# Projections taken term by term, and half of the values formed behind attention's first units

## The chip, the cores and the metric

The kernel runs on one core of a Trainium2 chip. Its time is the device time of one execution in microseconds. The engines are PE (matrix products), DVE and ACT (elementwise work, copies, exponentials), POOL (small elementwise work, indirect transfers) and SP (issues transfers). Each works through its own queue in order and waits on semaphores that the others raise.

## The reference, cut to what matters

Per image of 16: a layer norm, a convolutional channel attention, and then on its 1024 tokens of 192 channels the block that the change touches:

```python
qkv = jnp.einsum('btc,fc->btf', x, W_qkv)          # x: normalised tokens
wei = jnp.einsum('bqhd,bkhd->bhqk', q, k) * scale   # 6 heads of 32
wei = jnp.where(causal[None, None], wei, -jnp.inf)
wei = jax.nn.softmax(wei, axis=-1)
out = jnp.einsum('bhqk,bkhd->bqhd', wei, v).reshape(Bq, Tq, H * HS)
out = jnp.einsum('btf,cf->btc', out, W_proj) + b_proj
out = jnp.einsum('btf,cf->btc', out, W_proj) + b_proj
```

After the images, a mixture of four experts (two per token) runs over all tokens in blocks of 512 rows.

## The kernel before

Image by image, PE does the convolutions as matmuls over shifted copies (`ring`), the channel mixing of token blocks 0 to 7 into PSUM banks `k % 6`, and then attention. DVE adds a bias to each mixed block (`channel_mixed`, L1045, raises `y_sb`), takes statistics, and writes the normalised tokens `xhat`, blocks 0 to 3 in `normed(i, 0)`, 4 to 7 in `normed(i, 1)` (L1021). The fixed order on DVE is: `normed(i, 0)`, blocks 5 and 6 mixed, `low_channels(i, 0)`, block 7 mixed, `low_qk(i, 0)`, `normed(i, 1)`, the next two `low_qk`, `low_channels(i, 1)`, three more `low_qk`.

Precision comes from split operands. PE transposes the tokens (L1714); ACT copies the result as high parts `T0` and `T1` (L1458, raises `T_hi`), and DVE subtracts to get `T2` and the low rows of `T1` (`low_channels`, L1029 and L1032, raises `T_lo`). Every projection is a sum of five matmuls, `qkv` in the code: two on `T0`, one on `T2`, two on `T1`. There are six groups of 128 rows of queries and keys by 512 tokens (`queries_keys`, group `n` in bank `n % 4`; 0 to 2 are the first half of the tokens). Each is copied by ACT (`QKh`, L1551, raises `qk_hi`) and subtracted by DVE (`QKl`, `low_qk`, L1038, raises `qk_lo`). Loads issued by SP (`load_keys`) and POOL (`load_queries`) stack the parts into `KS` and `QS`. Group 1 writes bank 1, which mixed block 7 used, so from group 1 on the wait is for all eight blocks in `y_sb`.

Values are eight chunks of 128 tokens, five matmuls each (L1739), copied by ACT to `v_sb` (L1462, raises `v_done`); before, chunks 2 to 7 stand between the last group and the first score, in banks 6, 7, 4, 5 by turns.

Attention is 48 units, query chunk by query chunk, six heads each. For unit `n` PE computes the scores of unit `n + 3` (or `n + 2`), and then transposes the probabilities of unit `n` (L1782) in banks 4 and 5. DVE takes a row maximum of the scores (L1051), ACT the exponential with its row sums (L1469) and a copy of the transposed block (L1483). The first score waits for the last `qk_lo`, since scores use banks 0 to 3, and for the landed loads. The output matmuls of a query chunk (L1804) use banks 6 and 7. POOL scatters the rows of the image before (`send`, L780), issues the query loads (L357), adds a bias (`output_bias`, L786) and spreads the inverse row sums (`inverse_wide`, L728).

Of the kernel before, what the change touches and what calls it, by code (L numbers as in the profile page):

```python
# [15 lines left out]
P = 128  # L16
# [3 lines left out]
def hybrid_block_kernel(nc, x, ln_g, ln_b, conv_w, conv_bias_row, conv_taps, conv_bias, alpha_rows, w_f_t, b_f,  # L20
# [50 lines left out]
    with ExitStack() as ctx:  # L71
# [387 lines left out]
        def value_bank(k):  # L459
            return (6, 7, 4, 5)[k % 4]  # L460
# [189 lines left out]
        def _(pool):  # L650
# [138 lines left out]
            for i in range(B):  # L789
# [7 lines left out]
                if i:  # L797
                    send(i - 1, 5, 6)
# [7 lines left out]
                if i:  # L806
                    send(i - 1, 6, NC)
# [615 lines left out]
        def _(act):  # L1423
# [102 lines left out]
            for i in range(B):  # L1526
# [15 lines left out]
                for n in range(NQ):  # L1542
                    if n == QK_FIRST:
                        for k in range(2):
                            values_out(i, k)
                        high_channels(i, 1)
                    f, nh = QK_ORDER[n]
# [4 lines left out]
                for k in range(2, NC):  # L1552
                    values_out(i, k)
                for n, (qc, h) in enumerate(SOFT):
                    exponentials(i, n)
                    if n:
                        blocks_out(i, n - 1)
                    if qc and h == 2:
                        norms_out(i, qc - 1)
# [49 lines left out]
        def _(pe):  # L1609
# [110 lines left out]
            def queries_keys(i, n):  # L1720
                f, nh = QK_ORDER[n]
                if n >= 4:
                    pe.wait_ge(qk_lo, NQ * i + n - 3)
                if n < 4:
                    pe.wait_ge(y_sb, NC * i + min(NC - 1 + n, NC))
                for m, (act_part, w_part) in enumerate(qkv):
                    if f == 0 and m in (0, 3):
                        pe.wait_ge(T_hi, 4 * i + 2 * nh + 1 + m // 3)
                    if f == 0 and m in (2, 3):
                        pe.wait_ge(T_lo, 4 * i + 2 * nh + m - 1)  # L1730
                    last = t.matmul(bank(n % 4), w_part[:, P * f:P * (f + 1)],
                                    act_part[:, BANK * nh:BANK * (nh + 1)], start=m == 0, stop=m == 4)
                last.then_inc(qk_ps, 1)

            def values_of_tokens(i, k):
                if k >= 4:
                    pe.wait_ge(v_done, NC * i + k - 3)
# [5 lines left out]
            def passed(i, t):  # L1743

                if t < 2:
                    pe.wait_ge(v_done, NC * (i + 1))
# [100 lines left out]
            for i in range(B):  # L1847
# [35 lines left out]
                for n in range(QK_FIRST):  # L1883
                    queries_keys(i, n)
# [3 lines left out]
                for n in range(QK_FIRST, NQ):  # L1888
                    queries_keys(i, n)
                for k in range(2, NC):  # L1890
                    values_of_tokens(i, k)
                if not i:
# [3 lines left out]
                for n, (qc, h) in enumerate(SOFT):  # L1896
                    for m in SCORED[n]:
                        query_scores(i, m)
                    if n == NU - 1 and i + 1 < B:
# [173 lines left out]
```

## Time and profile before

| | us |
|---|---|
| median of 3 runs | 3336.41 |
| lowest, highest | 3331.54, 3340.59 |
| profiled execution | 3334.18 |
| its span, first to last instruction | 3332.3 |
| PE busy in the span | 3067.4 (92%) |
| DVE busy | 2202.3 (66%) |
| ACT busy | 1871.5 (56%) |
| POOL busy | 874.5 (26%) |

The images take the first two thirds of the span, the experts the rest. The mean granted clock is 0.984. Start times below count from the start of the span. A busy span of a matmul overlaps that of the next, so the pace of PE is read from start to start.

### The profile page before, as it was taken

The numbers are of one execution on the slowest core, as the hardware profiler recorded it, in microseconds if no ns is written. First come the engines' busy times: TensorE is split into PE (matmuls) and PEld (weight loads), VectorE is DVE, ScalarE is ACT, GpSimd is POOL, SyncE is SP. The second block draws the span as 40 slices with busy tenths as digits, with TensorE's granted clock in tenths as the row PEclk, the third lists the DMA queues.
The fourth block names the chain that finished last, engine by engine and source line by source line (L and its number), as shares of the span: only waits on it lengthen the run. The fifth ranks groups of instructions, "written<-read, shape, count | busy, mean of one in ns | idle before, by whom it ended". The sixth has DMA issues, their size and how long they took to land. (4 is left out here: it accounts for less than half of the span.)

```text
span 3332.3 us, 72396 instructions
## 1 busy us (share of the span) xinstructions
PE 3067.4 (92%) x26642; PEld 2344.2 (70%) x26642; DVE 2202.3 (66%) x5619; ACT 1871.5 (56%) x3996; POOL 874.5 (26%) x1142
## 2 busy tenths in 40 slices
PE   4999999999999999999999999958999999999995
PEld 1666667666666676666766766637888888888884
DVE  3777677677776776777767767664555655655653
ACT  0647456465474664654746647535555555555553
POOL 2121313303223133132230331450223223223222
PEclk9999999999999999999999999979999999999997
DMA  7546445454364454544644546515667767667673
GB/s 177 142 114 178 115 124 148 124 150 126 113 184 116 122 149 122 153 118 120 173 125 115 148 123 154 156 47 159 195 206 213 221 208 220 210 205 228 206 212 120
DMA packets 256516, 519.82 MB, mean 156 GB/s; under 512 B 70919, under 2 KB 161991, under 8 KB 246521
## 3 DMA queue, kind: packets, MB, share of 16 engines
q1 hardware_dynamic: 222878, 453.58, 48.6%
q0 software_dynamic: 29184, 59.81, 6.0%
q8 instruction: 217, 3.56, 0.4%
q10 hardware_dynamic: 4107, 1.81, 0.3%
q14 instruction: 130, 1.06, 0.1%
HBM read 242.82 MB, written 117.71 MB: 108 GB/s over the span
## 5 line engine op out<-in xcount | busy, mean ns | idle before, releaser
L1051 DVE TENSOR_REDUCE minus_max<-ps 128x1 f32<-128x128 f32 (+7 forms) x768 | 571.6, 750 | 243.7 <-PE ps L1772 232.3
L1469 ACT ACTIVATE p_sb<-ps,minus_max 128x128 f32<-128x128 f32 (+7 forms) x768 | 569.3, 741 | 41.3 <-DVE minus_max L1051 37.8
L1782 PE MATMUL ps<-ident,p_sb 128*128 128x128 f32 x3456 | 530.6, 279 | 44.2 <-ACT p_sb L1469 18.4
L1356 DVE TENSOR_TENSOR g_lo<-g,g_hi 128x512 fp32r<-128x512 f32 x402 | 282.8, 704 | 369.3 <-ACT g_hi L1593 369.3
L1592 ACT ACTIVATE g<-ps,bcur 128x512 f32<-128x512 f32 x402 | 276.6, 688 | 429.2 <-PE ps L1967 429.2
L1483 ACT ACTIVATE PT<-ps 128x512 f32<-128x512 f32 (+3 forms) x768 | 396.7, 517 | 132.7 <-PE ps L1782 123.5
L1782 PEld LDWEIGHTS ps<-ident,p_sb 128*128 128x128 f32 x3456 | 370.0, 141 | 99.4 <-ACT p_sb L1469 37.5
L1983 PE MATMUL ps<-w_all,g_hi 128*128 x1608 | 434.6, 351 | 0.0
L1770 PE MATMUL ps<-KS,QS 96*128 96x512 f32 (+3 forms) x1152 | 393.6, 401 | 21.4 <-ACT p_sb L1469 17.9
L1647 PE MATMUL ps<-ring,wconv 125*32 125x512 f32 (+1 forms) x3072 | 358.4, 606 | 15.0 <-DMA ring<-padded_scratch 15.0
L780 POOL DMA_INDIRECT routed_rows<-xhat,slot x256 | 253.3, 989 | 358.2 <-issue 358.2
L846 POOL DMA_INDIRECT got<-expert_rows,slot x256 | 257.6, 1006 | 333.6 <-issue 270.7
L728 POOL COPY inverse_wide<-inverse_sums 128x192 f32<-128x192 f32 x128 | 44.2, 345 | 1040.3 <-DVE inverse_sums L1072 1040.3
L1988 PE MATMUL ps<-w_all,g_lo 128*128 x1608 | 293.1, 264 | 0.0
L1988 PEld LDWEIGHTS ps<-w_all,g_lo 128*128 128x128 f32 x1608 | 289.4, 188 | 2.0
L1983 PEld LDWEIGHTS ps<-w_all,g_hi 128*128 128x128 f32 x1608 | 263.8, 191 | 22.8
L1593 ACT ACTIVATE g_hi<-ps,bcur 128x512 fp32r<-128x512 f32 x402 | 273.5, 680 | 0.0
L1967 PE MATMUL ps<-X_hi,cur 128*128 128x512 f32 x804 | 264.9, 411 | 7.5 <-ACT g_hi L1593 5.6
L1967 PE MATMUL ps<-X,cur 128*128 128x512 f32 x804 | 250.0, 392 | 0.0
L1770 PEld LDWEIGHTS ps<-KS,QS 96*128 96x128 f32 x1152 | 196.9, 195 | 69.4 <-ACT p_sb L1469 42.4
L1647 PEld LDWEIGHTS ps<-ring,wconv 125*32 125x32 f32 (+1 forms) x3072 | 94.2, 111 | 207.5 <-issue 192.7
L1064 DVE COPY PT<-ps 128x128 f32<-128x128 f32 (+3 forms) x384 | 184.9, 482 | 67.6 <-PE ps L1782 67.5
(276 smaller groups left out, 5442.5 us busy)
## 6 DMA issues: line engine op xcount, KB each, us to landing
ring<-padded_scratch SPq DMA_DIRECT2D x576, 204.0 KB
cur<-w_all SPq DMA_DIRECT2D x67, 1536.0 KB, 7.1
routed_rows<-zero_rows SPq DMA_DIRECT2D x67, 384.0 KB, 5.0
xgt<-routed_rows SPq DMA_DIRECT2D x67, 384.0 KB, 4.6
expert_rows<-y_rows SPq DMA_DIRECT2D x67, 384.0 KB, 3.0
padded_scratch<-xpad SPq DMA_DIRECT2D x32, 435.0 KB, 3.6
x_sb<-x SPq DMA_DIRECT2D x16, 768.0 KB, 5.5
KS<-QKh SPq DMA_DIRECT2D x128, 96.0 KB
```

Source lines behind the costliest of these rows:

```text
L1051: v.tensor_reduce(nmx[:, qc, h:h + 1], score_place(n), AX, ALU.max, negate=True).then_inc(mx_sb, 1)
L1356: v.tensor_tensor(g_lo[:, n % 2, :], g32[:, n % 2, :], g_hi[:, n % 2, :].bitcast(F32), ALU.subtract).then_inc(lo_sb, 1)
L1469: a.activation(p_sb[n % NP][:, 0:P * (qc + 1)], score_place(n), ACT.Exp, bias=nmx[:, qc, h:h + 1], accum_out=ls[:, qc, h:h + 1]).then_inc( ...
L1483: a.activation(PT[h][:, k0:k0 + nb, :], bank(pass_bank(t))[:, 0:P * nb].rearrange("p (k q) -> p k q", q=P), ACT.Copy).then_inc(PT_act, 1)
L1592: a.activation(g32[:, n % 2, :], bank(n % 2), ACT.Gelu, bias=b1)
L1593: a.activation(g_hi[:, n % 2, :], bank(n % 2), ACT.Gelu, bias=b1).then_inc(gelu_sb, 1)
L1647: last = t.matmul(bank(2 * (r % 2) + nh)[W * j:W * (j + 1), :], wconv[s][0:KROWS[s], h, c0:c0 + W], rhs, start=s == 0, stop=s == 1, skip_g ...
L1770: t.matmul(o[:, k0:k0 + keys], QS[0:96, qc // TPC, h, P * (qc % TPC):P * (qc % TPC + 1)], KS[0:96, h, k0:k0 + keys], start=True, stop=k0 + ...
L1782: last = t.transpose(bank(pass_bank(piece))[:, P * k:P * (k + 1)], p_sb[n % NP][:, P * (k0 + k):P * (k0 + k + 1)], ident[:, :])
L1967: last = t.matmul(bank(n % 2), w[:, W1L * part + P * j:W1L * part + P * (j + 1)], act_part[:, :], start=m == 0, stop=m == 4)
L1983: t.matmul(bank(acc_bank(r, tt))[:, 0:2 * C], g_hi[:, n % 2, P * tt:P * (tt + 1)], w2j, start=j == 0, stop=False, skip_group_check=True)
L1988: last = t.matmul(bank(acc_bank(r, tt))[:, 0:C], g_lo[:, n % 2, P * tt:P * (tt + 1)], w2j[:, 0:C], start=False, stop=j == J - 1, skip_grou ...
```

## The change

Three things move; nothing is added or removed in arithmetic. First, `queries_keys` takes a half of the tokens instead of a group: it issues the two `T0` terms of all three groups, then the `T2` term of all three, then the two `T1` terms of each. The second half comes behind the values of chunks 2 and 3. Second, the values of chunks 4 to 7 go behind the scores issued in attention units 0 to 3, on PE and on ACT, with banks 6 and 7 by turns. Third, POOL issues the scatter of block 5 behind the query loads and no longer ahead of them.

```diff
         def value_bank(k):
-            return (6, 7, 4, 5)[k % 4]
+            return 6 + k % 2
...
                 token_rstd(i, 1)
-                if i:
-                    send(i - 1, 5, 6)
                 pool.wait_ge(qk_hi, NQ * i + PAIR_GROUPS)
...
                 if i:
-                    send(i - 1, 6, NC)
+                    send(i - 1, 5, NC)
...
                         high_channels(i, 1)
+                        for k in range(2, TPC):
+                            values_out(i, k)
...
-                for k in range(2, NC):
-                    values_out(i, k)
                 for n, (qc, h) in enumerate(SOFT):
                     exponentials(i, n)
                     if n:
                         blocks_out(i, n - 1)
+                    if TPC + n < NC:
+                        values_out(i, TPC + n)
...
+            def queries_keys(i, nh):
+                group = range(QK_FIRST * nh, QK_FIRST * (nh + 1))
+
+                def term(n, m):
+                    f = QK_ORDER[n][0]
+                    act_part, w_part = qkv[m]
+                    return t.matmul(bank(n % 4), w_part[:, P * f:P * (f + 1)],
                                     act_part[:, BANK * nh:BANK * (nh + 1)], start=m == 0, stop=m == 4)
-                last.then_inc(qk_ps, 1)
+
+                pe.wait_ge(T_hi, 4 * i + 2 * nh + 1)
+                for n in group:
+                    if n >= 4:
+                        pe.wait_ge(qk_lo, NQ * i + n - 3)
+                    else:
+                        pe.wait_ge(y_sb, NC * i + min(NC - 1 + n, NC))
+                    term(n, 0)
+                    term(n, 1)
+                pe.wait_ge(T_lo, 4 * i + 2 * nh + 1)
+                for n in group:
+                    term(n, 2)
+                pe.wait_ge(T_hi, 4 * i + 2 * nh + 2)
+                pe.wait_ge(T_lo, 4 * i + 2 * nh + 2)
+                for n in group:
+                    term(n, 3)
+                    term(n, 4).then_inc(qk_ps, 1)
 
             def values_of_tokens(i, k):
-                if k >= 4:
-                    pe.wait_ge(v_done, NC * i + k - 3)
+                if k >= 2:
+                    pe.wait_ge(v_done, NC * i + k - 1)
...
                 if t < 2:
-                    pe.wait_ge(v_done, NC * (i + 1))
                     return
...
                 norm_transposes(i, 0)
-                for n in range(QK_FIRST):
-                    queries_keys(i, n)
+                queries_keys(i, 0)
                 for k in range(2):
                     values_of_tokens(i, k)
                 norm_transposes(i, 1)
-                for n in range(QK_FIRST, NQ):
-                    queries_keys(i, n)
-                for k in range(2, NC):
+                for k in range(2, TPC):
                     values_of_tokens(i, k)
+                queries_keys(i, 1)
...
                     for m in SCORED[n]:
                         query_scores(i, m)
+                    if TPC + n < NC:
+                        values_of_tokens(i, TPC + n)
```

PE, the first half of the projections in image 0, before. `T_128` is `T1`:

```order
L1731 MATMUL ps<-T_hi,wqkv_a_hi 128x512 [waits T_hi,y_sb]
L1731 MATMUL ps<-T_hi,wqkv_a_lo 128x512
L1731 MATMUL ps<-T_lo,wqkv_a_hi 128x512 [waits T_lo]
L1731 MATMUL ps<-T_128,wqkv_b_hi 128x512 [waits T_lo,T_hi]
L1731 MATMUL ps<-T_128,wqkv_b_lo 128x512
L1731 MATMUL ps<-T_hi,wqkv_a_hi 128x512 [waits y_sb]
```

The same place after:

```order
L1726 MATMUL ps<-T_hi,wqkv_a_hi 128x512 [waits y_sb,T_hi]
L1726 MATMUL ps<-T_hi,wqkv_a_lo 128x512
L1726 MATMUL ps<-T_hi,wqkv_a_hi 128x512 [waits y_sb]
L1726 MATMUL ps<-T_hi,wqkv_a_lo 128x512
L1726 MATMUL ps<-T_hi,wqkv_a_hi 128x512 [waits y_sb]
L1726 MATMUL ps<-T_hi,wqkv_a_lo 128x512
L1726 MATMUL ps<-T_lo,wqkv_a_hi 128x512 [waits T_lo]
L1726 MATMUL ps<-T_lo,wqkv_a_hi 128x512 x2
L1726 MATMUL ps<-T_128,wqkv_b_hi 128x512 [waits T_lo,T_hi]
```

The first matmul of the second group, with its wait for `y_sb`, moved from sixth place to third, ahead of every low part.

ACT at the start of attention in image 0, before; `v_sb` are the value chunks, `p_sb` the exponentials of units 0, 1 and so on, `PT` the transposed blocks:

```order
L1551 ACTIVATE QKh_157<-ps 128x512 [waits qk_ps] x3
L1462 ACTIVATE v_sb_118<-ps 128x192 [waits v_ps] x6
L1469 ACTIVATE p_sb0_130,row_sums_109<-ps,minus_max_108 128x128 [waits mx_sb]
L1469 ACTIVATE p_sb1_131,row_sums_109<-ps,minus_max_108 128x128 [waits mx_sb]
L1483 ACTIVATE PT0_160<-ps 128x128 [waits query_ld0_0,key_ld0_1,query_ld0_1,key_ld0_0,pT_ps]
L1469 ACTIVATE p_sb2_132,row_sums_109<-ps,minus_max_108 128x128 [waits mx_sb]
```

and after:

```order
L1551 ACTIVATE QKh_157<-ps 128x512 [waits qk_ps] x3
L1467 ACTIVATE p_sb0_130,row_sums_109<-ps,minus_max_108 128x128 [waits mx_sb]
L1460 ACTIVATE v_sb_118<-ps 128x192 [waits v_ps]
L1467 ACTIVATE p_sb1_131,row_sums_109<-ps,minus_max_108 128x128 [waits mx_sb]
L1481 ACTIVATE PT0_160<-ps 128x128 [waits query_ld0_0,key_ld0_1,query_ld0_1,key_ld0_0,pT_ps]
L1460 ACTIVATE v_sb_118<-ps 128x192 [waits v_ps]
L1467 ACTIVATE p_sb2_132,row_sums_109<-ps,minus_max_108 128x128 [waits mx_sb]
```

Four of the six copies of values stand one each ahead of the exponentials of units 1 to 4, and wait for the matmuls of the unit.

## Rows read from the trace of the kernel before

**Rows 1.** Busy time by stretch of image 5 (from:to, length, each engine's busy time).

```profile
777.00:796.00 19.00, 16.94 (x102) 13.49 (x102) 12.47 (x32) 10.99 (x36) 14.12 (x16) 1.00 0.58 164
...
840.00:893.00 53.00, 52.08 (x607) 30.61 (x599) 36.27 (x102) 27.01 (x48) 4.55 (x9) 1.00 0.39 118
```

**Rows 2.** Waits over the span: total us, times, longest.

```profile
PE ps L1731 <- DVE T L1032: 9.8, 31, 0.3
```

**Rows 3.** Timeline of PE, image 5: start, length, instruction, [idle before].

```profile
777.16 0.47 PE L1731 MATMUL ps<-T_hi,wqkv_a_hi 128*128 128x512 f32 x1 [0.34 <-DVE t_sb L1045]
777.47 0.40 PE L1731 MATMUL ps<-T_hi,wqkv_a_lo 128*128 128x512 f32 x1
...
779.37 0.39 PE L1731 MATMUL ps<-T,wqkv_b_lo 128*128 128x512 f32 x1
...
781.86 0.25 PE L1739 MATMUL ps<-wqkv_a_hi,T_hi 128*128 128x192 f32 x1
...
782.95 1.04 PE L1714 MATMUL ps<-ident,xhat 128*128 128x128 f32 x8
784.33 0.47 PE L1731 MATMUL ps<-T_hi,wqkv_a_hi 128*128 128x512 f32 x1 [0.34 <-ACT T_hi L1458]
...
788.62 0.25 PE L1739 MATMUL ps<-wqkv_a_hi,T_hi 128*128 128x192 f32 x1
...
791.96 0.24 PE L1770 MATMUL ps<-KS,QS 96*128 96x128 f32 x1
```

**Rows 4.** Timeline of DVE, the same stretch.

```profile
778.22 0.69 DVE L1032 TENSOR_TENSOR T<-ps,T 64x512 fp32r<-64x512 f32 x1
778.94 0.36 DVE L1045 TENSOR_TENSOR t_sb<-ps,bf_bc 128x196 f32<-128x196 f32 x1
...
780.42 0.69 DVE L1038 TENSOR_TENSOR QKl<-ps,QKh 128x512 fp32r<-128x512 f32 x1 [0.30 <-ACT QKh L1551]
781.28 1.35 DVE L1021 TENSOR_SCALAR xhat<-t_sb,tmv,rstd 128x192 f32<-128x192 f32 x4 [0.17 <-POOL rstd L716]
...
789.46 0.69 DVE L1038 TENSOR_TENSOR QKl<-ps,QKh 128x512 fp32r<-128x512 f32 x1 [0.45 <-ACT QKh L1551]
```

**Rows 5.** Timeline of ACT, the same stretch.

```profile
779.79 0.60 ACT L1551 ACTIVATE QKh<-ps 128x512 fp32r<-128x512 f32 x1 [2.29 <-PE ps L1731]
...
783.15 0.33 ACT L1462 ACTIVATE v_sb<-ps 128x192 f32<-128x192 f32 x1 [0.23 <-PE ps L1739]
...
795.25 0.36 ACT L1469 ACTIVATE p_sb<-ps,minus_max 128x128 f32<-128x128 f32 x1
...
795.60 0.28 ACT L1483 ACTIVATE PT<-ps 128x128 f32<-128x128 f32 x1
795.77 0.47 ACT L1469 ACTIVATE p_sb<-ps,minus_max 128x256 f32<-128x256 f32 x1
```

**Rows 6.** Timeline of PE, attention's first units in image 5.

```profile
792.46 0.30 PE L1770 MATMUL ps<-KS,QS 96*128 96x128 f32 x1
...
793.14 0.33 PE L1782 MATMUL ps<-ident,p_sb 128*128 128x128 f32 x1 [0.31 <-ACT p_sb L1469]
...
795.75 0.33 PE L1782 MATMUL ps<-ident,p_sb 128*128 128x128 f32 x1
...
796.37 0.38 PE L1770 MATMUL ps<-KS,QS 96*128 96x256 f32 x1
```

**Rows 7.** Timelines of SP's queue and of POOL, image 5.

```profile
785.29 1.46 SPq L351 DMA_DIRECT2D KS<-QKl  x2
...
782.88 0.96 POOL L780 DMA_INDIRECT routed_rows<-xhat,slot  x1 [0.30 <-issue]
783.84 2.29 POOL L357 DMA_DIRECT2D QS<-QKh  x4
...
797.45 0.34 POOL L728 COPY inverse_wide<-inverse_sums 128x192 f32<-128x192 f32 x1 [2.00 <-DVE inverse_sums L1072]
```

**Rows 8.** Loads of `KS` issued from 780 to 800 us: time to landing.

```profile
DMA to landing us min/median/max: 2.6/3.6/4.2
```

More of the change, by code:

```diff
@@ L1718, in _ @@
             qkv = ((T0, wqa_hi), (T0, wqa_lo), (T2, wqa_hi), (T1, wqb_hi), (T1, wqb_lo))
[L1720 to L1731, printed above, removed]
-                                    act_part[:, BANK * nh:BANK * (nh + 1)], start=m == 0, stop=m == 4)
-                last.then_inc(qk_ps, 1)
+            def queries_keys(i, nh):
[4 more added lines that the diff above has]
+                    return t.matmul(bank(n % 4), w_part[:, P * f:P * (f + 1)],
+                                    act_part[:, BANK * nh:BANK * (nh + 1)], start=m == 0, stop=m == 4)
+                pe.wait_ge(T_hi, 4 * i + 2 * nh + 1)
[14 more added lines that the diff above has]
+                    term(n, 4).then_inc(qk_ps, 1)
             def values_of_tokens(i, k):
-                if k >= 4:
-                    pe.wait_ge(v_done, NC * i + k - 3)
+                if k >= 2:
+                    pe.wait_ge(v_done, NC * i + k - 1)
                 for m, (act_part, w_part) in enumerate(qkv):
```

## The prediction

> **What bounds the kernel now.** I read the share of busy time by stretch first. In one of the 16 images (image 5, counted from 0; its cycle is some 133.3 us) PE is busy 52.08 of 53.00 us in the late attention, but only 16.94 of 19.00 us where queries, keys and values are formed and attention begins [rows 1]. All of the change lies there. The granted clock is 1.00 in both, the 2.4 GHz level, so the clock plays no part. I then followed that stretch engine by engine in the timelines. The 16 images repeat each other: the wait of a projection for the subtraction that writes `T`, for one, stands there 31 times with 0.3 us as the longest [rows 2]. So I work out one image and multiply by 16. What follows the first six units is a closed loop of PE, ACT and DVE and then the PE-bound part, with no spare time ahead of a fixed event. A delay at the sixth unit's transpose (795.75) is therefore passed on whole. I measure the change at that point.
>
> **Part 1: the first three groups, term by term.** Before, the five matmuls of group 0 start at 777.16, and their last at 779.37; it waits for the low part and again for `T`. From there matmuls follow each other every 2.49/11 = 0.226 us to 781.86 [rows 3]. Fifteen unhindered ones would take 3.4 us and not 4.70, so about 1.2 us is what the new order is after. But the second group now comes third in PE's queue, not sixth. It writes bank 1, which token block 7 used, so it waits for `y_sb` to say that all eight blocks were read. The last read is on DVE's row at 778.94 (0.36 us, ends 779.30), and DVE does it behind both low parts, 778.22 to 778.91 being the second [rows 4]. Before, group 1 came at about 779.6, when that was over. Now PE does two matmuls (777.16, 777.47) and stands until 779.36 (a hop between engines I take at 0.06, where ACT's end at 780.39 to DVE's 780.42 shows 0.03), and then both low parts have long been there. From 779.36: one first step of 0.31 us (as 777.16 to 777.47) and 12 of 0.226 end at 782.38, against 781.86. The stall has not gone; it has moved to another wait, and all three terms that could have filled it are queued behind it. **+0.52 us.**
>
> **Part 2: what the first result's lateness does.** Group 0's last matmul now starts 8 steps after 779.36, at 781.25. ACT copied it 0.42 us after that start (779.37 to 779.79) and took 0.60 [rows 3, 5]: now 781.67 to 782.27, 1.9 us later. DVE subtracts it for 0.7 us (780.42), and *behind this subtraction* stand the four subtractions of the normalised tokens 4 to 7, 1.35 us, which before started at 781.28 and waited for POOL alone [rows 4]. Now: 782.30 + 0.69, less 0.04 by which neighbours on DVE overlap, is 782.95; end 784.30. PE's second eight transposes wait for them: 784.36 instead of 782.95 [rows 3]. They take about 0.88 (1.04 less the overlap of the last). Values of chunks 2 and 3 come next: ten matmuls at 3.34/30 = 0.111 us (788.62 to 791.96) are 1.11, ending 786.35; they cover the copies and low parts of the second half, so its 0.84 us of stalls (784.33 to 788.62 is 4.29 for 15 x 0.23) do go. Its 15 matmuls end at 789.76. Before, PE had by 788.62 all groups and two values chunks behind it, and at 789.73 would have had two more, the same work. So up to here the change wins nothing: **0 us** within 0.1.
>
> **Part 3: no cover in front of the scores.** The first score waits for the last low part of the keys, since it writes the same banks. Before, six chunks of values (3.34 us) covered copy and subtraction: the last subtraction was at 789.46 (0.69) and the scores at 791.96, with no wait. Now the three groups finish close together: copies of 0.60 each from 789.04 end at 790.84, subtractions of 0.69 each from 789.67 end at 791.74, and the scores start at 791.80. PE stands idle for 2.0 us in one piece. **-0.16 us** against before, instead of the 2.23 us that the removal of four chunks seems to give.
> The operands would not be later. SP issues its key loads as soon as the copies of the first three groups are there, now some 0.6 us later; its last issues of this wave ended at 785.29 + 1.46, and landing takes 2.6 to 4.2 us [rows 7, 8], so 786.75 + 0.6 + 4.2 = 791.6 at most here. POOL passes two scatters fewer ahead of the query loads at 783.84 [rows 7], which go some tenths earlier for it. The two scatters (0.30 + 0.96 each) come on top behind them, 2.5 us against the 2.00 that POOL idled ahead of `inverse_wide` at 797.45 and the 1.5 us by which the sums it waits for move back [rows 7]. Cost 0, price if that cover fails below.
>
> **Part 4: four chunks of values behind units 0 to 3.** In a unit before, ACT does an exponential, reads its sum and copies a transposed block: 795.25 to 795.77 is 0.52 us, and PE idles between [rows 5]. PE's transpose follows the start of the exponential by 0.50 (795.25 to 795.75) [rows 5, 6]. Now each unit has 0.56 us of matmuls in front of its transpose and a copy of 0.33 us *in front of the next exponential*. So a ring forms. If PE's five matmuls end at E, their last started at E - 0.11. ACT's copy starts 0.31 after that (as 783.15 is after 782.84, the last step ahead of 782.95) [rows 3, 5], at E + 0.20. The exponential starts 0.22 later (a short ACT instruction starts about 0.1 before the end of the one ahead: 795.60 + 0.28 to 795.77), and the next transpose is at E + 0.92. PE's own work is less: 0.11 for a transpose, 0.19 for a score, 0.56, together 0.86. Walked through from 791.80: four scores to 792.49 (the fourth started 0.50 after the first, 791.96 to 792.46), values to 793.05, and there transpose 0 (its exponential would allow 792.98, as 791.96 to 793.14 before). Unit 1: values end at 793.05 + 0.86 = 793.91, but the transpose waits for the ring, 793.05 + 0.92 = 793.97. Unit 2: 793.97 + 0.86 = 794.83, the ring gives the same. Unit 3: its score has 256 columns and takes 0.08 more (0.38 against 0.30), so 795.77 [rows 3, 6]. Transpose 4 is at 795.77 + 0.92 = 796.69, and transpose 5 at + 0.52 = 797.21. Before it was at 795.75. **+1.62 us** from the scores on, since 3.79 us before (791.96 to 795.75) held, beside five transposes' and nine scores' worth of steps, only some 1.4 us of idle PE for 2.24 us of matmuls, and the ring adds the rest.
>
> **Sum.** Per image 797.21 - 795.75 = +1.46 us; 16 images +23.4 us. The profiled execution took 3334.2 us (span 3332.3), which gives 3357.6. The median shown is 2.2 us above it, which gives 3359.8; I say 3359, between them.
> The unknown costs: a ring step is not in the trace as such. Its floor is PE's 0.86 (-0.2 us per image), its ceiling, with the 0.08 that a first matmul after a wait costs more (0.31 for 0.23) and a hop more, about 1.0 to 1.05 (+0.5). DVE or DMA neighbours can shift the scores by -0.3 to +0.4. Together +0.9 to +2.3 us per image, 14 to 37 us.
> The Trainium skill ("Perfetto Trace Analysis", Optimization Strategy) says that work of regimes bound by different engines may gain from being interleaved; that is the case for this change, and by it the values would lie in the idle time of the first units, the third rival below. The rows speak against it here, since the interleaved values need ACT, the engine that is full there.
>
> **The rivals.**
> *No early stall (same).* If the wait for block 7 does not bite, groups 0 to 2 end at 780.65, the low-part queue stays as before (tokens at 781.28), PE's second transposes come at 782.7, and by the steps of parts 2 and 3 the scores are at 790.1. The ring then gives transpose 5 at 795.5, -0.2 us per image: 3333. Against it: the order of DVE's rows and the bank numbers leave no way round it.
> *Late operands (slower still).* If key or query loads, squeezed against the second half's traffic, land 1 us after the scores are ready, or POOL is late for `inverse_wide`, +1 us per image comes on top: 3375. It decides once the last landing passes 791.8; my bound is 791.6, so it is near.
> *Values in idle time (faster).* No stall for block 7, and ACT's copies slip in without holding the exponentials. From 790.1, PE's own work to transpose 5 is 0.69 + 2.24 + five transposes (0.55) and five more scores (1.2), about 4.7 us: 794.8, -1.0 us per image, 3320. It needs both, and the rows show ACT back to back.
>
> **Chances.** Forecast 0.78, late operands 0.08, no early stall 0.09, values in idle time 0.05. About 0.3% (10 us) is what a measurement of this kernel can tell from no change. The forecast's own range is 3348 to 3373 and holds some nine tenths of its 0.78. The late operands reach to 3375. I take 3346 to 3374. Slower by over 0.3% is 0.78 + 0.08 less a little that a small ring leaves inside: 0.85. Same is 0.10, faster 0.05.
>
> **What would show it.** In the profile after: in each image a wait of some 1.6 us of the third projection matmul for DVE's `t_sb`; a wait of about 1.4 us at the second transposes' `xhat`, part of it for PE idle (0.8 to 0.9 us); 2.0 us of PE idle ahead of the first score, released by `QKl`; transposes of units 0 to 3 some 0.9 us apart and ACT's value copies right ahead of exponentials. PE's work is unchanged and its span longer. The prediction is wrong if the third matmul follows at 0.23 us, if the second transposes start as soon behind the last values as before (782.95, no idle), or if the distance from the first score to the sixth unit's transpose stays near 3.8 us.

## The result, and the profile after

| | us |
|---|---|
| before, median of 5 (lowest to highest) | 3336.41 (3331.54 to 3340.59) |
| changed, median of 5 (lowest to highest) | 3391.28 (3388.66 to 3392.88) |
| ratio, 95% interval | 1.0164, 1.0150 to 1.0178 |
| forecast (range) | 3359 (3346 to 3374) |

Slower, as forecast, but by 55 us and not by 23: the time lies 17 us above the range. First the page of the changed kernel, beginning with its span and the busy time of PE:

```profile
span 3390.9 us, 72364 instructions
...
PE 3083.3 (91%) x26642; PEld 2369.5 (70%) x26642; DVE 2195.6 (65%) x5619; ACT 1861.7 (55%) x3996; POOL 875.3 (26%) x1142
```

PE has the same 26642 instructions as before and is busy 16 us longer (3083.3 against 3067.4). That is the first sign that something other than waiting was added. The mean granted clock of the profiled executions fell from 0.984 to 0.973.

The two waits that the forecast named are there. Waits over the span of the changed kernel: total us, times, longest.

```profile
PE ps L1726 <- DVE t_sb L1043: 29.1, 32, 1.5
PE ps L1780 <- DVE QKl L1036: 27.3, 16, 1.7
PE ps L1714 <- DVE xhat L1019: 25.6, 32, 2.2
```

The first is the third projection matmul's wait for token block 7 (of 32 entries, 16 are the long ones). The second is the idle ahead of the first score, 16 times 1.7 us. The third is that of the transposes of normalised tokens, 10.9 us in all before. Its longest entries, some 2 us, stand ahead of an image's first transposes, where the forecast put nothing.

Image 9 is the one of the 16 in which, counted from its first transpose, nothing but the forecast's mechanisms is at work. (The 1.98 us of idle ahead of that transpose are no part of the forecast; they belong to the third thing below.) PE's timeline there: start, length, instruction, [idle before]. It answers to [rows 3] and [rows 6].

```profile
1343.55 1.09 PE L1714 MATMUL ps<-ident,xhat 128*128 128x128 f32 x8 [1.98 <-DVE xhat L1019]
1345.03 0.47 PE L1726 MATMUL ps<-T_hi,wqkv_a_hi 128*128 128x512 f32 x1 [0.39 <-DVE t_sb L1043]
1345.34 0.40 PE L1726 MATMUL ps<-T_hi,wqkv_a_lo 128*128 128x512 f32 x1
1347.18 0.50 PE L1726 MATMUL ps<-T_hi,wqkv_a_hi 128*128 128x512 f32 x1 [1.45 <-DVE t_sb L1043]
...
1352.09 1.09 PE L1714 MATMUL ps<-ident,xhat 128*128 128x128 f32 x8 [0.57 <-DVE xhat L1019]
...
1359.42 0.33 PE L1780 MATMUL ps<-KS,QS 96*128 96x128 f32 x1 [1.70 <-DVE QKl L1036]
...
1360.82 0.27 PE L1792 MATMUL ps<-ident,p_sb 128*128 128x128 f32 x1
...
1361.76 0.33 PE L1792 MATMUL ps<-ident,p_sb 128*128 128x128 f32 x1
...
1362.65 0.28 PE L1792 MATMUL ps<-ident,p_sb 128*128 128x128 f32 x1
...
1363.58 0.33 PE L1792 MATMUL ps<-ident,p_sb 128*128 128x128 f32 x1
...
1364.48 0.33 PE L1792 MATMUL ps<-ident,p_sb 128*128 128x128 f32 x1 [0.38 <-ACT p_sb L1467]
...
1364.99 0.33 PE L1792 MATMUL ps<-ident,p_sb 128*128 128x128 f32 x1
```

The same place in image 5 of the kernel before begins with

```profile
775.73 1.09 PE L1714 MATMUL ps<-ident,xhat 128*128 128x128 f32 x8 [0.66 <-DVE xhat L1021]
```

Counted from the image's first transpose (775.73 before, 1343.55 here), the forecast's points and the measured ones are:

| point | before | forecast | image 9 after |
|---|---|---|---|
| third projection matmul | | 3.63 | 3.63 |
| second transposes | 7.22 | 8.63 | 8.54 |
| first score | 16.23 | 16.07 | 15.87 |
| sixth unit's transpose | 20.02 | 21.48 | 21.44 |

So the sum of the forecast holds to 0.04 us, and with it the ring: the transposes are 0.94, 0.89, 0.93 and 0.90 apart, for 0.92. That it is as close as 0.04 is luck in part: the first score came 0.20 early, and from it to the sixth transpose it took 5.57 us for 5.41. The other images are later. In image 5, which the forecast worked out, the sixth transpose is at 815.30, 23.03 behind its first at 792.27. PE's timeline and the table by stretch (from:to, length, busy PE, PE load, DVE, ACT, POOL, granted clock, DMA share, GB/s) show why:

```profile
792.27 1.09 PE L1714 MATMUL ps<-ident,xhat 128*128 128x128 f32 x8 [0.77 <-DVE xhat L1019]
...
795.89 0.59 PE L1726 MATMUL ps<-T_hi,wqkv_a_hi 128*128 128x512 f32 x1 [1.45 <-DVE t_sb L1043]
796.28 0.63 PE L1726 MATMUL ps<-T_hi,wqkv_a_lo 128*128 128x512 f32 x1
796.71 0.63 PE L1726 MATMUL ps<-T_hi,wqkv_a_hi 128*128 128x512 f32 x1
...
799.88 0.40 PE L1726 MATMUL ps<-T,wqkv_b_lo 128*128 128x512 f32 x1
```

```profile
792.20:795.80 3.60, 1.79 (x10) 1.15 (x10) 3.44 (x11) 1.08 (x2) 1.65 (x2) 1.00 0.16 55
795.80:800.40 4.60, 4.50 (x13) 3.54 (x14) 0.78 (x5) 0.56 (x2) 2.24 (x3) 0.63 0.12 43
```

Behind the stall PE's steps are 0.43 us (796.28 to 796.71) instead of 0.23, and the mean granted clock of this part is 0.63: for most of it 0.5, the 1.2 GHz level, then 1.00 again, 2.4 GHz. The stretch at the lower level, a *low stretch* from here on, is 3.41 us long and costs some 1.5 us (the sixth transpose at 22.9 to 23.0 where an image has one, for 21.44). In image 6 it comes twice over, in the other place, behind the idle ahead of the scores:

```profile
943.00:946.30 3.30, 1.60 (x9) 1.06 (x7) 1.89 (x3) 1.57 (x3) 2.56 (x3) 1.00 0.86 256
946.30:953.00 6.70, 6.70 (x36) 6.61 (x36) 2.13 (x7) 2.99 (x14) 4.13 (x4) 0.50 0.88 229
```

Up to the last image's attention the changed kernel spends the time of 26 such stretches at the lower level (6.8 us counted as two), the kernel before that of 5; 4 of each lie ahead of the first image's first transposes. Of the 22 others of the changed kernel, 21 lie between an image's first transposes and its sixth unit. The mean delay of the sixth transpose is 3.2 us per image instead of 1.46. The images together are 51.7 us longer, from the first image's first transpose to the last one's, of 58.6 us in the span.

A third thing is in POOL's queue. The forecast costed the moved scatters at 0. (`rstd` is the small POOL operation that DVE needs before it can write `xhat`.) In image 6 of the changed kernel, POOL just ahead of the first transposes:

```profile
921.37 0.96 POOL L780 DMA_INDIRECT routed_rows<-xhat,slot  x1 [4.94 <-issue]
922.63 0.96 POOL L780 DMA_INDIRECT routed_rows<-xhat,slot  x1 [0.30 <-issue]
...
926.43 0.97 POOL L780 DMA_INDIRECT routed_rows<-xhat,slot  x1 [0.30 <-issue]
927.42 1.04 POOL L716 TENSOR_TENSOR rstd<-rstd,minus_half 128x4 f32<-128x4 f32 x1
```

DVE there:

```profile
925.60 0.17 DVE L1010 TENSOR_SCALAR rstd<-tmv 128x4 f32<-128x4 f32 x1
...
928.57 1.47 DVE L1019 TENSOR_SCALAR xhat<-t_sb,tmv,rstd 128x192 f32<-128x192 f32 x4 [2.14 <-POOL rstd L716]
```

and POOL in image 8 of the kernel before:

```profile
1172.16 0.96 POOL L780 DMA_INDIRECT routed_rows<-xhat,slot  x1 [0.30 <-issue]
1174.11 1.04 POOL L716 TENSOR_TENSOR rstd<-rstd,minus_half 128x4 f32<-128x4 f32 x1 [0.99 <-DVE rstd L1012]
```

Before, POOL's last scatter ended a microsecond ahead of `rstd`, and POOL waited for DVE. After, a scatter stands 4.94 us behind its predecessor, the following ones end with `rstd` already due (DVE's part of it was there at 925.77), and the whole image waits for POOL. That is image 6; in others, as image 5, the two only touch. The place of the gap moved as well. Of the six scatters ahead of `rstd`, in images 2 to 14, three passed before it in the kernel before (gap 1.9 to 2.8 us), and only the first does now (3.2 to 4.9 us), so five scatters and not three stand between the gap and `rstd`. PE's idle ahead of an image's first transposes, 0.6 to 0.7 us in images 1 to 15 before, is 1.3 to 2.2 us in five of them now.

### The profile page after: what moved, and what is told of

It reads as the page before. It is cut to its first block and busy times, and to the rows that moved or that the text cites. A ratio compares the mean times of both kernels' runs of the same rounds, so it can differ in the third digit from the quotient of the medians.

```text
span 3390.9 us, 72364 instructions
## 1 busy us (share of the span) xinstructions
PE 3083.3 (91%) x26642; PEld 2369.5 (70%) x26642; DVE 2195.6 (65%) x5619; ACT 1861.7 (55%) x3996; POOL 875.3 (26%) x1142
## 3 DMA queue, kind: packets, MB, share of 16 engines
q8 instruction: 217, 3.56, 0.4%
## 5 line engine op out<-in xcount | busy, mean ns | idle before, releaser
L1993 PEld LDWEIGHTS ps<-w_all,g_hi 128*128 128x128 f32 x1608 | 263.7, 190 | 22.9
```

Source lines behind the costliest of these rows:

```text
L1993: t.matmul(bank(acc_bank(r, tt))[:, 0:2 * C], g_hi[:, n % 2, P * tt:P * (tt + 1)], w2j, start=j == 0, stop=False, skip_group_check=True)
```

## The experiments

The revised theory had three terms: the forecast's sum (a), the stretches at 1.2 GHz (b) and POOL's order (c). The rival was that (b) and (c) are by-products of the other changes and nothing is gained by removing them, or that the forecast's mechanisms had been priced too low. All ratios are to the kernel before, with 95% intervals. The kernel before, measured again beside these runs, had medians of 3338.05, 3336.38 and 3335.90 us, so a difference of 2 us between two experiments says nothing. In the expectations "half clock" stands for a low stretch. Times inside an image are counted from its first transpose, in images without a low stretch unless it is said; stretches are counted in the one profiled execution, up to the last image's attention.

**The bank wait alone.** Only the bank numbers of the groups differ, so that group 0 to 2 need nothing of block 7; the group that takes its bank is the fourth.

```diff
+        QK_BANK = (0, 2, 3, 1, 0, 2)
...
-                    a.activation(QKh[:, f, BANK * nh:BANK * (nh + 1)], bank(n % 4), ACT.Copy).then_inc(qk_hi, 1)
+                    a.activation(QKh[:, f, BANK * nh:BANK * (nh + 1)], bank(QK_BANK[n]), ACT.Copy).then_inc(qk_hi, 1)
...
-                        pe.wait_ge(y_sb, NC * i + min(NC - 1 + n, NC))
+                        pe.wait_ge(y_sb, NC * i + (NC if n == 3 else NC - 1))
```

> The changed kernel with one thing different: the six groups of queries and keys lie in banks 0, 2, 3, 1, 0, 2 instead of 0, 1, 2, 3, 0, 1, so that no group of the first half needs token block 7 to have been read (the wait for all eight blocks stands at the fourth group). Theory A (the wait for block 7 costs the early part, and each stretch of half clock that a stall brings costs about 1.5 us): the third projection matmul follows the second at 0.23 us, the second eight transposes come 7.0 us after the first ones and not 8.5 to 10.1, the first score after 14.4 us and not 15.9 to 17.5, and transpose 5 after 19.8 us at full clock. The 2.0 us of idle PE ahead of the first score stay, and some images still fall to the half clock behind it. 3334 us with no half clock, 3334 + 16 x 1.5 = 3358 with one stretch in each image. Rival B (the early wait only hides other waits, low parts or loads, that then take its place): scores stay at 15.9 us or later, time above 3375.

Measured: 3360.94 (3359.02 to 3364.05), ratio 1.0069 (1.0052 to 1.0086): 30 us faster than the changed kernel. The third matmul moved from 3.63 to 2.02, the sixth transpose from 21.44 to 20.46. That is 0.98 us per image, 16 us; six stretches fewer (20 instead of 26) at 1.5 us are 9 more, and some 5 us are not accounted for. The bank wait was real, and it cost 30 us, 1.9 per image, which is more than its own 1.45 us of idle. Theory A had the direction and the third matmul right and was too low in the rest: second transposes at 7.5 and not 7.0, first score at 14.9 and not 14.4, time 3 us above its 3358. With POOL's order as before (further below) the second transposes do come at 6.96.

**Filling the two idle times.** In the stall for block 7 PE does six, and ahead of the first score eight, matmuls of 512 columns into bank 4, where nobody reads their result. This adds work and changes no wait.

```diff
+            def filler(nh, count):
+                for _ in range(count):
+                    t.matmul(bank(4), wqa_hi[:, 0:P], T0[:, BANK * nh:BANK * (nh + 1)], start=True, stop=True)
...
+                    if n == 1:
+                        filler(0, 6)
...
                 queries_keys(i, 1)
...
+                filler(1, 8)
```

> The changed kernel with 14 matmuls of 512 columns more in each image, whose results nobody reads: six into bank 4 in front of the second group's wait for block 7, eight into bank 4 between the last group and the first score. They lie in the idle time of PE and change no dependency. Theory A (a third to a half of the loss comes from the clock, which falls to its half level behind the idle stretches): stretches at half clock in the image part go from 20 to a few, and the time falls to 3345 to 3370, transpose 5 at 21.4 to 21.6 us in nearly all images. Rival C (the clock falls for another reason, or the loss is all in the dependencies): 3391 or more, since PE has 14 x 0.23 x 16 = 51 us more work.

Measured: 3372.06 (3367.66 to 3374.95), ratio 1.0105 (1.0088 to 1.0122). With 14 more matmuls per image the kernel is 19 us *faster*, and 2 us above the expected range. The stretches fell from 26 to 8, and the sixth transpose stands at 21.4 to 21.5 in 12 of 16 images. This shows term (b): the idle time brings the low stretch, and the low stretch is what costs. Of the 8 that are left, 4 lie ahead of the first image's first transposes; those in images 5, 7 and 13 begin right behind 1.64, 2.00 and 2.01 us of idle ahead of the first transposes, which is POOL's late `rstd`. So term (c) brings low stretches too.

**Values ahead of the scores again.** Chunks 2 to 7 behind the second half, all ahead of the scores, in their old banks; term by term, the bank wait and POOL's changed order stay.

```diff
-                for k in range(2, TPC):
+                queries_keys(i, 1)
+                for k in range(2, NC):
                     values_of_tokens(i, k)
-                queries_keys(i, 1)
...
-                    if TPC + n < NC:
-                        values_of_tokens(i, TPC + n)
```

> The changed kernel with the values put back: chunks 2 to 7 behind the last group and ahead of the first score, in banks 6, 7, 4, 5 by turns, as before. What stays is the order term by term with its wait for block 7, and POOL's order. Theory A: the second half's groups start at 785.8 us on the clock of image 5 of before instead of 784.3, and the scores some 0.7 us later than before, with values in front of them and no idle PE there. 3336 + 11 = 3347 without half clock; half clock in the first group of about half the images (the stall of 1.6 us stays) adds 8 x 1.5 = 12 us, so 3347 to 3360. Rival D (the values behind the units are the whole loss): 3325 to 3340.

Measured: 3368.31 (3361.75 to 3375.87), ratio 1.0090 (1.0066 to 1.0115); sixth transpose at 20.58, or 22.2 to 22.5 in the five images with two stretches, 18 stretches. Both expectations missed: 8 us above the 3347 to 3360 of theory A, and far above rival D's. Theory A left out POOL's order, which is priced further below.

**The values' move without the term order.** Groups one by one as before, values of chunks 4 to 7 behind the units.

```diff
-                queries_keys(i, 0)
+                for n in range(QK_FIRST):
+                    queries_keys(i, n)
...
-                queries_keys(i, 1)
+                for n in range(QK_FIRST, NQ):
+                    queries_keys(i, n)
```

> The changed kernel with the projections put back group by group (five terms of one group, then the next), so the wait for block 7 does not bite. What stays: values of chunks 2 and 3 ahead of the second half, chunks 4 to 7 behind units 0 to 3, POOL's order. Theory A: first part as before (second transposes after 7.2 us), scores after about 14.5 us, if the loads have landed by then, which landed between 14.0 and 15.4 us before; transpose 5 5.4 us after the first score, after 19.9 to 20.6 us: 3334 to 3345 without half clock, and with a stretch of it behind the idle time ahead of the scores 3350 to 3370. Rival D (the ring of values and exponentials is the whole loss, the early wait nothing): 3375 to 3391.

Measured: 3360.65 (3353.39 to 3363.41), ratio 1.0062 (1.0042 to 1.0082); scores at 14.8, sixth transpose 20.37, or 21.8 with a stretch, 17 stretches. This is inside theory A's 3350 to 3370. Either part alone, with POOL's change, costs 23 to 30 us over the kernel before, and the two together 55. The next pair takes POOL's change by itself.

**POOL's order alone, and its undoing.** The first is the kernel before with only the scatter of block 5 behind the query loads; the second is the changed kernel with it ahead again.

```diff
                 token_rstd(i, 1)
-                if i:
-                    send(i - 1, 5, 6)
...
-                    send(i - 1, 6, NC)
+                    send(i - 1, 5, NC)
```

> The kernel before with the third part of the change alone: POOL issues the two scatters of block 5 behind the query loads. Theory P (in each kernel with this order POOL's next image shows its second scatter 4.6 us behind the first and the last one ending where the first normalisation's rstd should start, so that in some images rstd is late by 1.2 to 1.4 us): one third to one half of the images are longer by 1.2 to 1.4 us and the others by 0.2, together +5 to +12 us, 3342 to 3350. Rival Q (POOL's order has nothing to do with that gap): as before, 3338, with the last scatters of a batch 5.2 us ahead of the transposes as in the kernel before.

> The changed kernel with POOL's order put back (two scatters of block 5 ahead of the query loads). Theory P: the late rstd goes, some 7 us less, 3380 to 3386; the query loads then are issued 0.5 us later than in the changed kernel, which costs nothing as the scores wait for QKl. Rival Q: 3391, the gap behind the first scatter stays.

Measured: alone 3354.78 (3350.32 to 3362.28), ratio 1.0058 (1.0039 to 1.0078), 18 us for two moved scatters per image, 5 us above what theory P allowed; undone in the changed kernel 3382.81 (3381.20 to 3386.01), ratio 1.0143 (1.0122 to 1.0164), 8.5 us back, as expected. The waits of DVE for `rstd`, in the kernel before and with POOL's order alone:

```profile
DVE xhat L1021 <- POOL rstd L716: 12.4, 31, 0.8
```

```profile
DVE xhat L1019 <- POOL rstd L716: 28.8, 31, 2.0
```

16.4 us more in the very wait, and the longest went from 0.8 to 2.0. Ahead of the first transposes it is longer by 0.6 to 1.5 us in seven images and by 0.2 or less in the others; at the second ones it is longer in most images, and the sixth transpose stands at 20.36 for 20.06. The clock adds to it: this kernel has 13 low stretches for 5, and 8 of them begin right behind idles of 1.73 to 2.06 us ahead of the first transposes, in images 6, 8, 9, 11 and 13. PE in image 8, where the steps behind such an idle are 0.42 us:

```profile
1183.02 1.09 PE L1712 MATMUL ps<-ident,xhat 128*128 128x128 f32 x8 [2.00 <-DVE xhat L1019]
...
1187.34 0.63 PE L1729 MATMUL ps<-T_hi,wqkv_a_hi 128*128 128x512 f32 x1
1187.76 0.63 PE L1729 MATMUL ps<-T_hi,wqkv_a_lo 128*128 128x512 f32 x1
```

In the profiled executions, 25.6 us apart, 8 stretches at 1.5 us are some 12. So the parts do not add: with POOL's 18 us taken off, the term order costs some 12 us and the values' move some 4, together 35 of the 55.

**Values between, ahead of the scores.** Term by term, banks exchanged, chunks 2 and 3 ahead of the second half and 4 to 7 behind it, ahead of the scores; once with POOL's order as changed and once as before.

```diff
                 for k in range(2, TPC):
                     values_of_tokens(i, k)
                 queries_keys(i, 1)
+                for k in range(TPC, NC):
+                    values_of_tokens(i, k)
...
-                    if TPC + n < NC:
-                        values_of_tokens(i, TPC + n)
```

> Term by term with the first half free of block 7 (banks 0, 2, 3, 1, 0, 2), values of chunks 2 and 3 ahead of the second half as in the changed kernel, but chunks 4 to 7 directly ahead of the first score, as before, in banks 6 and 7; POOL's order as changed. Theory A (a stall that is filled counts, cover ahead of the scores is needed, the ring behind the units costs): the last subtraction ends after 14.4 us, values end at about the same time, first score after 14.6 us instead of 16.2, transpose 5 after 18.4 instead of 20.0, -1.6 us per image; no half clock in the attention start. With POOL's late rstd (+7): 3338 - 26 + 7 = 3319; if loads land after 15 us it is 3325 to 3332. Rival B (loads or low parts take the place of what is removed): 3338 or more.

> The same with POOL's order as before the change. Theory P and A together: 3338 - 26 = 3312 if the query loads, which stand behind two scatters, land before 14.6 us; they landed between 13.4 and 15.4 us before, which then were some tenths early, so in some images the first score waits up to 0.8 us: 3312 to 3325. If the query loads decide, this kernel is slower than the one with POOL's order changed.

Measured: 3332.30 (3325.81 to 3347.56), ratio 0.9998 (0.9982 to 1.0014); with POOL's order as before 3311.10 (3309.00 to 3312.07), ratio 0.9925 (0.9905 to 0.9945). The first missed theory A's 3319: its sixth transpose is at 19.17 and not 18.4, and its times scatter by 22 us, which stays unexplained. The second beats both kernels, by 25 us the one before. PE in image 11 of it:

```profile
1575.07 0.27 PE L1753 MATMUL ps<-wqkv_b_lo,T 128*128 128x192 f32 x1
1575.18 0.25 PE L1783 MATMUL ps<-KS,QS 96*128 96x128 f32 x1
...
1578.98 0.33 PE L1795 MATMUL ps<-ident,p_sb 128*128 128x128 f32 x1
```

The score follows the last value without a gap, the sixth transpose is 3.80 us behind it (3.79 before, [rows 3, 6]), and stands 18.59 behind the image's first: 1.4 us sooner than before. So term by term gains once no bank holds it up and four chunks cover the copies: 1.4 us of the 2.0 us of stalls that it set out to fill. In images 5, 10 and 15 the first score waits 0.67, 0.35 and 0.20 us for a query load (`DMA QS<-QKl`), so the loads are now nearly what bounds it. The waits of the transposes for `xhat` in this pair, POOL's order changed and as before:

```profile
PE ps L1715 <- DVE xhat L1020: 37.2, 32, 2.0
```

```profile
PE ps L1717 <- DVE xhat L1022: 22.4, 32, 1.6
```

14.8 of the 15.3 us between the two profiled executions (3325.81 and 3310.54) stand in this one wait; the medians are 21 us apart.

**Both suspects removed from the changed kernel.** The fillers and POOL's order as before, together.

> The changed kernel with fourteen extra matmuls of 512 columns per image in PE's two idle times (their result is not used) and the scatter of block 5 ahead of the query loads again. My theory is that the changed kernel is slower by three terms: the late first three groups and the ring (the forecast's +1.46 us per image), the half-clock stretches, and POOL's order. With both of the last two taken away, what is left must be the forecast: the filled kernel had 3372.1 us, POOL's order gave 8.5 us in the changed kernel and 18 in the kernel before, so 3354 to 3364 us, with the sixth transpose at 21.45 us behind the image's first. Rival: if something not yet named holds the changed kernel back, it stays at 3368 us or more.

Measured: 3359.67 (3354.87 to 3360.70), ratio 1.0066 (1.0046 to 1.0087). The forecast, which had neither of the two terms, was 3359. PE's steps behind the stall are again those at 2.4 GHz, and the granted clock there is 1.00. Timeline and table of image 5:

```profile
785.84 1.55 PE L1724 MATMUL ps<-T_hi,wqkv_a_hi 128*128 128x512 f32 x6
787.44 0.50 PE L1732 MATMUL ps<-T_hi,wqkv_a_hi 128*128 128x512 f32 x1
787.78 0.40 PE L1732 MATMUL ps<-T_hi,wqkv_a_lo 128*128 128x512 f32 x1
788.02 0.39 PE L1732 MATMUL ps<-T_hi,wqkv_a_hi 128*128 128x512 f32 x1
```

```profile
783.80:792.00 8.20, 7.52 (x39) 5.91 (x39) 5.76 (x18) 3.07 (x7) 6.01 (x7) 1.00 0.19 62
```

The sixth transpose stands at 21.68 to 21.75 in most images, 0.2 later than forecast, since the second ones come at 8.78 and not 8.63; 7 stretches are left. From the first image's first transpose to the last one's it is 24.1 us longer than before, for a forecast of 15 x 1.46 = 22. With the fillers in, POOL's order is worth 12.4 us (3372.06 to 3359.67); with POOL's order back, the fillers are worth 23.1 (3382.81 to 3359.67), and 15 stretches fewer (22 to 7) at 1.5 us are 22.5. The two terms together are 31.6 us, and what stays without them is the forecast's time within 1 us.

**The place of the values, with banks and POOL's order mended.** Term by term, banks exchanged, POOL's order as before, values of chunks 4 to 7 behind the units; the second kernel lets DVE copy them instead of ACT.

```diff
+            def values_out(i, k):
+                dve.wait_ge(v_ps, NC * i + k + 1)
+                v.tensor_copy(v_sb[:, k, :], bank(value_bank(k))[:, 0:C]).then_inc(v_dve, 1)
```

> Term by term, with the banks exchanged so that nothing waits for token block 7, values of chunks 4 to 7 behind the units, POOL's order as before the change. It differs from the version with all values ahead of the scores (3311.1 us) in the place of chunks 2 to 7 alone. Theory (the place behind the units costs, by the 2 us of idle ahead of the scores, the ring and the half clock behind it): with POOL's order changed the same step was 3360.9 against 3332.3, 28.6 us, so here 3336 to 3345 us. Rival (the place of the values is free once the banks are exchanged, and what differed was how POOL met it): 3311 to 3320 us.

> As the one before, but DVE and not ACT copies the values of chunks 4 to 7, so ACT's exponentials have nothing more ahead of them. The forecast's ring (ACT's copy ahead of the exponential, 0.92 us a unit) says that PE's own work of 0.86 us then sets the step: 4 x 0.06 = 0.24 us per image, 4 us in all, and with the transposes of units 0 to 4 some 0.86 us apart. Rival (ACT's copies are the whole of what the place costs, the values lying in idle time without them): back to 3315 us, transposes 0.6 to 0.7 us apart. Second rival: DVE's copy delays the maxima of later scores and it is as slow as or slower than the one before.

Measured: 3361.42 (3351.72 to 3371.40), ratio 1.0071 (1.0049 to 1.0093), and with DVE's copies 3348.18 (3331.67 to 3363.72), ratio 1.0037 (1.0013 to 1.0061). The first missed both of its expectations: 50 us above the version with the values ahead of the scores, not 25 to 34. It has 27 low stretches against 5. (Its expectation speaks of chunks 2 to 7; only chunks 4 to 7 stand elsewhere.) PE at its first scores in image 5:

```profile
797.52 0.33 PE L1783 MATMUL ps<-KS,QS 96*128 96x128 f32 x1 [1.70 <-DVE QKl L1039]
...
798.12 0.45 PE L1783 MATMUL ps<-KS,QS 96*128 96x128 f32 x1 [0.19 <-DMA QS<-QKl]
798.37 0.33 PE L1785 MATMUL ps<-mask_rows_q,ident_bf 128*128 128x128 bf16 x1
798.46 0.46 PE L1783 MATMUL ps<-KS,QS 96*128 96x128 f32 x1
```

The first score is the earliest of the kernels so far, 14.31 behind the first transpose. But the second is 0.60 behind it instead of 0.20, since its query load has only just landed, and PE is already at the lower level. This is the forecast's "late operands": the loads bind where the scores are early enough, here in images 1 and 13 at the first score too. That the second gap is why more low stretches come here than with POOL's order changed (27 against 20) fits, but no run isolates it.

In the second kernel, image 5 (its first transpose at 781.10), the transposes follow PE's own work:

```profile
797.10 0.27 PE L1802 MATMUL ps<-ident,p_sb 128*128 128x128 f32 x1
...
797.94 0.27 PE L1802 MATMUL ps<-ident,p_sb 128*128 128x128 f32 x1
...
798.78 0.27 PE L1802 MATMUL ps<-ident,p_sb 128*128 128x128 f32 x1
...
799.67 0.27 PE L1802 MATMUL ps<-ident,p_sb 128*128 128x128 f32 x1
...
799.97 0.28 PE L1802 MATMUL ps<-ident,p_sb 128*128 128x128 f32 x1
```

They are 0.84, 0.84 and 0.89 apart instead of 0.9 and more, and the fifth comes 0.30 behind the fourth, since no copy of a value stands ahead of its exponential. From the first transpose to the sixth it is 3.56 us for 4.17. So the ring through ACT was a real part, 0.6 us per image (10 us) and not the expected 0.24: the expectation counted four steps and forgot the fifth, which has no values on PE at all but had ACT's last copy ahead of it. The medians differ by 13 us. The two kernels' times scatter by 20 and 32 us, and their stretches are 27 and 19, so the medians say less here than the timeline does. The theory's 4 us and its rival's return to 3315 both missed. The rest of what the place costs, to the 3311 of the version between, would be the idle ahead of the scores and the clock behind it; no run with fillers was made in this version to show it.

## Why the prediction was right or wrong

- **Part 1, the stall for block 7: right.** Third matmul at 3.63, as forecast, 1.45 us of idle. Exchanging three banks took it away.
- **Part 2, the second transposes: right.** 8.54 for 8.63 at full clock.
- **Part 3, the idle ahead of the scores: right**, in one piece of 1.70 us for 2.0, released by `QKl` in all 16 images, and right that the scores come hardly sooner (15.87 for 16.07, before 16.23).
- **Part 4, the ring: right.** 0.92 us a unit, sixth transpose at 21.44 for 21.48 (with two small errors that cancel, as said above), and taking ACT out of it gave PE's own 0.84 to 0.89.
- **"The granted clock is 1.00 in both, the 2.4 GHz level, so the clock plays no part": this step failed.** It read the clock of a stretch that the change was about to alter. The forecast itself put two single idle times of 1.6 and 2.0 us into each image, where the stalls before were short and many, and did not ask what the clock does behind them. It fell to 0.5 for 3.41 us, 26 times up to the last image's attention instead of 5. By the runs this is worth 19 us (fillers added to the changed kernel) to 23 us (fillers added with POOL mended). The term was not mis-sized but missing, and the range had nothing for it.
- **"Cost 0" for POOL's two scatters: this step failed too.** The cover that it named, the idle ahead of `inverse_wide`, did hide them, in the image in which they were issued (POOL still idled 2.15 us there in image 5). The cost arose elsewhere: in the next image the scatters behind the first came later, and `rstd`, which shares the queue, was late. The step followed the moved transfers to the next wait on POOL, but not round to the next image. Worth 8.5 to 12.4 us in the changed kernel, and 18 alone, a part of it again through low stretches behind the new idle. Why the gap in POOL's queue moved stays open.
- Of the rivals, "late operands" gave the nearest time (3375) by the wrong mechanism: in the changed kernel every first score is released by `QKl`, 16 of 16. It turned up in versions whose scores come sooner. "Values in idle time" had the wrong sign for this placing. ACT full, the reason given, is a part of it, 0.6 us per image or 10 us; the rest is the missing cover ahead of the scores and the clock. The Trainium skill ("Perfetto Trace Analysis", Optimization Strategy) says that interleaving regimes with different most-contended engines may improve performance; for this placing it did not: 3361 us with the values behind the units, 3311 us with them ahead of the scores.

The 0.85 for slower was right. The range, 3346 to 3374, was built from the errors of the known terms alone and left no room for effects that the trace of before could not show: ahead of the first transposes of images 1 to 15 it has no idle of more than 0.7 us.

## What to carry to other kernels

A wait that ends up in one piece can cost more than its own length: a single idle of 1.45 us on PE was followed in half of the images by 3.41 us at 1.2 GHz, and filling it with useless matmuls made the kernel faster. So an order that removes several short stalls and makes a long one must be charged for the clock as well. Before independent work is moved away from in front of a dependent step, ask what covers the copies then; here the same term order, with four chunks of values kept as cover, the banks chosen so that no group waits for block 7, and POOL's queue left as it was, is 0.75% faster than before instead of 1.6% slower. And a transfer that is moved in a queue shared with a small, urgent operation is to be followed round the loop, into the next iteration.

## What the runs showed of the hardware

- Stretches at a granted clock of 0.5 were 3.41 us long, or 6.7 and more where they followed each other, right behind PE idle times of 1.45 and 1.70 us in the changed kernel, and of 1.64 to 2.06 us with the fillers in or with POOL's order alone, with PE busy on both sides. They did not come each time: image 9 had both idle times and none of the stretches. What decides in which images they come stays open. The Trainium skill ("TensorE: Matmul & The Clock Gate", A second HAM failure mode: psum-queue depth-cycling) says that frequent short idles between groups of matmuls can make the clock go back and forth between its levels; the time of 21 stretches inside the images, behind idles of 1.45 to 1.75 us, agrees with it.
- At that level the steps were 0.43 us for a matmul of 512 columns (0.23 at full clock) and 0.21 for one of 192 columns (0.11), and a stretch cost some 1.5 us.
- A scatter of POOL takes 0.96 us and the next one 0.30 us more to start, but in images 2 to 14 one of the six ahead of `rstd` stood much further behind its predecessor: the fourth, by 1.9 to 2.8 us, in the kernel before, and the second, by 3.2 to 4.9 us, with the changed order, with nothing shown that it waited for. Why the order of the queue in the image before changes this gap was not settled.
